# A graph layer on one core: the node features of every fifth group are loaded during the edge stage

## What is computed

```python
h = silu(edge_scalars @ Wfc1/4);  w = h @ Wfc2/8             # 192 weights per edge
e0, e1 = (x0 @ Wl1_0)[src], (x1 @ Wl1_1)[src]                # gathered source nodes
mid    = products of w, e0, e1 and the edge's 4 harmonics     # per edge
mean   = segment_sum(mid, dst) / max(count, 1)               # per node
conv   = mean @ Wl2_s, mean @ Wl2_v;  alpha = mean @ Wa
y      = x @ Wsc * node_vec1 + alpha * conv
out    = layernorm(x + y)                                    # 160 features per node
```

## Time and profile before

| | |
|---|---|
| median of 3 runs | 924.31 us (922.17 to 926.71) |
| the profiled execution's own time | 922.11 us |
| its span, first to last instruction | 920.4 us |
| busy: PE, DVE, ACT, POOL | 855.8, 808.2, 626.2, 714.1 us |
| data moved | 186.77 MB, mean 203 GB/s |
| edge stage, node stage | about 0 to 552 us, 552 to 920 us |

### The profile page before, as it was taken

One profiled execution on the slowest core, in us unless ns is written; L12 is line 12 of the kernel. 1 busy time (PEld: TensorE's weight loads), 2 busy tenths in 40 slices (PEclk: granted clock), 3 DMA queues, 4 the chain that ended last, 5 costly groups with the idle time before them and its releaser, 6 DMA issues.

```text
span 920.4 us, 32660 instructions
## 1 busy us (share of the span) xinstructions
PE 855.8 (93%) x10688; PEld 726.3 (79%) x10688; DVE 808.2 (88%) x2797; ACT 626.2 (68%) x1961; POOL 714.1 (78%) x804
## 2 busy tenths in 40 slices
PE   2999899999999999999999899989999999999994
PEld 1778778888877888888888778878888888888884
DVE  3788999999998999999999978888889898888897
ACT  1555555555555555555565546978988898888897
POOL 6777777777777776777777406989999998898995
PEclk9999999999999999999999999999999999999998
DMA  6465544544565555456544316999999999999994
GB/s 180 122 167 170 160 132 130 143 133 127 142 115 154 159 168 152 131 159 174 160 136 131 99 77 189 302 308 292 311 309 317 319 320 310 302 313 307 327 309 159
DMA packets 87539, 186.77 MB, mean 203 GB/s; under 512 B 17646, under 2 KB 48138, under 8 KB 87371
## 3 DMA queue, kind: packets, MB, share of 16 engines
q1 hardware_dynamic: 48411, 87.72, 29.4%
q10 hardware_dynamic: 20016, 61.15, 19.8%
q0 software_dynamic: 18944, 35.81, 17.7%
HBM read 119.66 MB, written 64.95 MB: 201 GB/s over the span
## 4 chain that ended last, share of the span: by engine, by line
PE 42%; DVE 14%; DMA 13%; issue 13%; SPq 9%; POOL 6%; ACT 1%; DVEq 0%; ACTq 0%; POOLq 0%
DMA win<-rows 10%; SPq L436 8%; PE ps L795 7%; PE ps L736 6%; POOL gat L587 6%; PE ps L715 5%; PE ps L733 4%; PE ps L696 4%; PE ps L702 4%; DVE mid L984 3%; DMA gat<-spread,srcs 3%; PE ps L678 3%; DVE z L1002 3%; PE ps L676 2%; PE ps L811 2%
## 5 line engine op out<-in xcount | busy, mean ns | idle before, releaser
L587 POOL DMA_INDIRECT gat<-turned,srcs x196 | 191.5, 977 | 67.0 <-issue 62.9
L587 POOL DMA_INDIRECT gat<-spread,srcs x196 | 188.2, 960 | 61.8 <-issue 59.1
L862 ACT ACTIVATE e_sb<-ps 128x512 f32<-128x512 f32 x196 | 106.4, 595 | 124.1 <-PE ps L702 124.1
L795 PE MATMUL ps<-win,hot 60*128 60x162 f32 x2352 | 189.1, 306 | 1.3 <-DVE hot L1325 1.1
L736 PE MATMUL ps<-wy,mid 128*128 128x161 f32 x784 | 182.3, 314 | 0.0
L795 PEld LDWEIGHTS ps<-win,hot 60*128 60x128 f32 x2352 | 165.0, 186 | 17.7 <-issue 12.1
L650 POOL TENSOR_TENSOR res<-agg,pre 128x640 f32<-128x640 f32 x98 | 151.8, 1549 | 30.7 <-ACT agg L907 30.4
L1008 DVE SCALAR_TENSOR_TENSOR msg<-ps,sha,z 128x161 f32<-128x161 f32 x392 | 151.0, 385 | 14.0
L907 ACT ACTIVATE agg<-ps,coef 128x160 f32<-128x160 f32 x392 | 124.7, 423 | 31.0 <-DVE coef L1365 30.3
L733 PE MATMUL ps<-wy,mid 128*128 128x97 f32 x784 | 141.4, 262 | 0.2 <-DVE mid L984 0.2
L984 DVE TENSOR_TENSOR mid<-ps,e_sb 128x512 f32<-128x512 f32 x196 | 133.1, 680 | 2.1 <-PE ps L715 2.1
(11 more groups left out here) (104 smaller groups left out, 1500.4 us busy)
## 6 DMA issues: line engine op xcount, KB each, us to landing
win<-rows SPq DMA_DIRECT2D x392, 114.6 KB, 4.1
rows<-msg SPq DMA_DIRECT2D x98, 326.0 KB
out<-fin ACTq DMA_DIRECT2D x47, 640.0 KB, 6.6
xin<-x_g ACTq DMA_DIRECT2D x92, 322.0 KB, 5.2
gat<-turned,srcs POOLq DMA_INDIRECT x196
gat<-spread,srcs POOLq DMA_INDIRECT x196
eas<-ea_t SPq DMA_DIRECT2D x7, 384.0 KB, 5.1
xin<-x_g SPq DMA_DIRECT2D x6, 322.0 KB, 4.1
```

The costliest lines, as they stand in the source:

```text
L587: pool.indirect_dma_start(out=gat[:, slot, first:first + of.shape[1]], out_offset=None, in_=of, in_offset=bass.IndirectOffsetOnAxis(ap=src ...
L795: last = nc.tensor.matmul(agg_ps[b1][:, 2 * h + k, 0:SW], hot[side(h), b1, k, c, :], win[side(h), (b - 1) % RING, k, c, 0:SW], start=c == ...
L862: nc.scalar.activation(e_sb[:, t, :], e_ps[:, t], ACT.Copy).then_inc(e_out[t], 1)
```

## The change

The x of every fifth group (g = 4, 9, ..., 94; 19 groups) gets a place of its own, `kept_x`, and is loaded by SP in the edge stage, one group at each i from 22 to 40, after the stores of that i. Other groups go on through the ring of six places of `xin`, counted by their rank among the groups that are not kept; ACT issues no x load in the step of a kept group. The space comes from laying node-stage tiles on edge-stage ones: `xa`, `hot`, `agg` and `xt` on `eas`, `res` and `pre` on `gat`, `fin` on the new tile `te`, which holds `t_sb` and `e_sb`. The edge-stage tables that lay in `res` and `fin` now lie in `kept_x`. No instruction of PE, DVE or POOL is added, removed or moved; POOL waits once for all kept loads (`kept_in`).

```diff
+KEEP = 5
...
+    KEPT = NG // KEEP
...
-        xa = sb("xa", [P, 2, GROUP + 1, P])
-        hot = sb("hot", [P, 2, 2, WC_ROWS, P])
-        agg = sb("agg", [P, 2, GROUP, D])
-        xt = sb("xt", [P, 2, GROUP + 1, P])
-        pre = sb("pre", [P, 2, GROUP, D])
-        res = sb("res", [P, RING, GROUP, D])
-        fin = sb("fin", [P, RING, GROUP, D])
+        kept_x = sb("kept_x", [P, KEPT, GROUP, XW])
...
+        def is_kept(g):
+            return g % KEEP == KEEP - 1
+
+        def rank(g):
+
+            return g - (g + 1) // KEEP
+
+        def of_rank(r):
+            return r + r // (KEEP - 1)
+
+        def x_tile(g):
+            return kept_x[:, g // KEEP] if is_kept(g) else xin[:, rank(g) % X_RING]
...
+            def keep_nodes(n):
+                sp.dma_start(kept_x[:, n].rearrange("p k w -> p (k w)"),
+                             block_rows(x_g, KEEP * n + KEEP - 1)).then_inc(kept_in, 16)
...
+                if 0 <= i - STARTS // 2 < KEPT:
+                    keep_nodes(i - STARTS // 2)
...
-                    n = (RING * i + b) % X_RING
-                    pool.wait_ge(x_in[n], 16 * ((RING * i + b) // X_RING + 1))
+                    g = RING * i + b
+                    x = x_tile(g)
+                    if is_kept(g):
+                        pool.wait_ge(kept_in, 16 * KEPT)
+                    else:
+                        pool.wait_ge(x_in[rank(g) % X_RING], 16 * (rank(g) // X_RING + 1))
...
-                if group_alive(i, b, 2) and group_alive(i, b, 2 - X_RING):
...
+                g = RING * i + b - 2
+                if group_alive(i, b, 2) and not is_kept(g) and of_rank(rank(g) + X_RING) < NG:
```

More of the change, by code:

```diff
@@ L109, in gnn_kernel @@
     CH = 4
-    assert NB - 1 >= WINDOWS + RING > EARLY + RING and WINDOWS > FLAG // 2 + 4 and NG // RING > 2 and NG % 2 == 0 and T <= 512 and NT < CH * P
+    KEPT = NG // KEEP
+    assert KEPT <= NB - 1 - STARTS // 2 and NB - 1 >= WINDOWS + RING > EARLY + RING and WINDOWS > FLAG // 2 + 4 and NG // RING > 2 and NG % 2 == 0 and T <= 512 and NT < CH * P
     inv8, inv32 = MUL0 ** -0.5, MUL1 ** -0.5
@@ L204, in gnn_kernel, with scratch @@
         shift = sb("shift", [P, RING, GROUP])
-        def scratch(tile, first, dims, dt=F32):
-            flat = tile[:].rearrange("p g k w -> p (g k w)")[:, first:first + dims[0] * dims[1]]
+        def scratch(first, dims, dt=F32):
+            flat = kept_x[:].rearrange("p g k w -> p (g k w)")[:, first:first + dims[0] * dims[1]]
             return flat.bitcast(dt).rearrange("p (a b) -> p a b", b=dims[1])
[L211 to L215, removed]
+        seq = scratch(0, (2, T), I32)
+        greater = scratch(2 * T, (1, T)).squeeze(1)
+        picked = scratch(3 * T, (CH, P), I32)
+        picked_below = scratch(3 * T + CH * P, (CH, P))
+        below = scratch(3 * T + 2 * CH * P, (CH, T))
+        t_sb = te[:, 0:12 * P].rearrange("p (b c k e) -> p b c k e", b=2, c=3, k=2)
+        e_sb = te[:, 12 * P:20 * P].rearrange("p (t e) -> p t e", t=2)
+        eas_flat = eas[:].rearrange("p b e -> p (b e)")
+        gat_flat = gat[:].rearrange("p n w -> p (n w)")
+        xa_at, hot_at = 0, 2 * (GROUP + 1) * P
+        agg_at = hot_at + 4 * WC_ROWS * P
+        xt_at = agg_at + 2 * GROUP * D
+        xa = eas_flat[:, xa_at:hot_at].rearrange("p (b k e) -> p b k e", b=2, k=GROUP + 1)
+        hot = eas_flat[:, hot_at:agg_at].rearrange("p (b k c e) -> p b k c e", b=2, k=2, c=WC_ROWS)
+        agg = eas_flat[:, agg_at:xt_at].rearrange("p (b k w) -> p b k w", b=2, k=GROUP)
+        xt = eas_flat[:, xt_at:xt_at + hot_at].rearrange("p (b k e) -> p b k e", b=2, k=GROUP + 1)
+        res = gat_flat[:, 0:RING * GROUP * D].rearrange("p (b k w) -> p b k w", b=RING, k=GROUP)
+        pre = gat_flat[:, RING * GROUP * D:(RING + 2) * GROUP * D].rearrange(
+            "p (b k w) -> p b k w", b=2, k=GROUP)
+        fin = te[:, 0:RING * GROUP * D].rearrange("p (b k w) -> p b k w", b=RING, k=GROUP)
         t_ps = ps[:, 0:2, 0:3 * P].rearrange("p k (c e) -> p k c e", e=P)
@@ L316, in gnn_kernel @@
         x_in = [sem(f"x_in{n}") for n in range(X_RING)]
+        kept_in = sem("kept_in")
         win_in = [sem(f"win_in{b}") for b in range(RING)]
@@ L418, in store_messages, with load_nodes @@
                     ).then_inc(messages_out[half], 16)
[L420 to L423, removed]
+            def load_nodes(r):
+                sp.dma_start(xin[:, r].rearrange("p k w -> p (k w)"), block_rows(x_g, of_rank(r))
+                             ).then_inc(x_in[r], 16)
+            def keep_nodes(n):
+                sp.dma_start(kept_x[:, n].rearrange("p k w -> p (k w)"),
+                             block_rows(x_g, KEEP * n + KEEP - 1)).then_inc(kept_in, 16)
             def load_windows(i, b):
@@ L1305, in step @@
                 scaling = group_alive(i, b, 5) and RING * i + b - 5 < NG - 3
-                nodes = (RING * i + b - 2) % X_RING
+                x = x_tile(RING * i + b - 2) if adding else None
                 g = groups(i, b, 2)
@@ L1352, in step @@
                         last = nc.vector.tensor_tensor(
-                            pre[:, b0, :, n:n + w], sc, xin[:, nodes, :, 1 + n:1 + n + w],
+                            pre[:, b0, :, n:n + w], sc, x[:, :, 1 + n:1 + n + w],
                             ALU.add)
```

18 lines of the change are left out of this document (8 added, 10 removed).

## The result

The changed kernel takes 917.49 us (median of 20 runs, 912.79 to 926.23), the kernel before 925.95 us (20 runs, 922.17 to 930.86). The ratio is 0.9925, with a 95% interval of 0.9902 to 0.9947. By it the changed kernel is 7 us faster (5 to 9); the two medians differ by 8.5 us. Forecast were 13.8 us (a ratio of 0.985).

What follows compares the result with a forecast made beforehand. The prediction took DMA bytes (3.52 us a group), just above PE's 3.45, to bound the node stage. A 14.3 us gain there less 0.5 us in the edge stage gave -13.8, from 924.3 to 910.5 us; range 906.0 (less 0.5) to 920.6.

Steps and rivals of the forecast that it cites:

- What remains of the stalls: Node stage: stalls left after the change, bounded by nothing and 6 us, taken as 4 us, for a gain of 14.3.
- DMA's is 3.52 us at best: Node stage: a group's 1127 kB at 320 GB/s need 3.52 us, against PE's own pace of 3.45 us.
- 13.8 us of ring against 4.1 us of landing: Node stage: a four-group window ring, 13.8 us at PE's pace, should carry 0.3 us, as windows land in 4.1 us (median).
- SP's short waits for PE: Node stage: SP waits for PE only 20.2 us in 322, so it issues windows soon after places come free.
- The first rival: Node stage: stalls are of latency, not bytes; only 3.7 us gained (920.6 us), or up to twice that; chance 0.20.
- The sentence at the end of the prediction: Node stage: prediction most wrong if engines fully busy at 320 GB/s merely had much queued, not because they could do no more.
- The edge stage: Edge stage: 19 added x loads cost nothing, or one wait of about 2.5 us at i = 22; 0.5 us taken.
- The lead of 8.7 us: Edge stage: a later gather ended 8.7 us before DVE took it, without a wait; most kept loads fall into that stretch.
- The tiles' new places: Node-stage tiles laid on edge-stage ones: no wait added, nothing counted, 1 us to either side for the turn between stages.
- ACT's 19 issues: Node stage: ACT issues 19 DMAs fewer, but at 3.26 of 3.45 us it does not end last; nothing counted.
- POOL as the next bound: Node stage, a rival: POOL's chain packs only into 3.53 us, losing 7.7 us, for 918 us; chance 0.06.
- The cap of 18.3 us: Node stage: the stalls are worth at most 18.3 us, as below that PE holds the pace at 3.45 us a group.

Runs made afterwards that it cites:

- e5: Changed kernel with no x loads in the node stage after groups 0 to 5; later groups all read group 4's x; ratio to the kernel before 0.9851.
- e11: Changed kernel storing only 32 of 1280 columns (16 KB, not 640 KB) for the first 94 groups; ratio to the kernel before 0.9808.
- e1: The changed kernel run once more, unedited, for a second trace; ratio to the kernel before 0.9931.
- e4: Changed kernel with one kept x load, at i = 30, in place of 19; all kept groups read it; ratio to the kernel before 0.9925.
- e13: Kernel before, nothing kept, with each group's output stored by itself and POOL waiting for the last label copy; ratio to the kernel before 0.9855.
- e3: Changed kernel making the 19 kept loads, but its node stage loads every group's x through the ring as before; ratio to the kernel before 1.0002.
- e14: Changed kernel with single stores, POOL waiting for the last label copy and kept loads at i = 24 to 42, second run; ratio to kernel before 0.9853.
- e9: Kernel before, nothing kept, with each group's output stored by itself (320 KB a step); ratio to the kernel before 0.9883.
- e2: Changed kernel with the kept loads issued two i later, at i = 24 to 42; ratio to the kernel before 0.9898.
- e7: Changed kernel with POOL making the first two groups' scaled x only after DVE's last edge-stage label copy; ratio to the kernel before 0.9889.

## Why the prediction was wrong

**The step that failed** is "What remains of the stalls": 4 us, between nothing and 6. Five traces show 12.7 us in the mean (7.3 to 18.8), so the node stage gained 5.5 us, not 14.3. The two bounds were both made of bytes over a rate, and the pace that they rest on, "DMA's is 3.52 us at best", was a reading of a busy share of 1.00 as a ceiling. In its place the runs show a path of 7.0 us, from PE's freeing of a place to DVE's copy, that SP's issuing and the landing share. The prediction had two things wrong in it. It set 13.8 us of ring against 4.1 us of landing, where 7.0 us were there and 2.7 of them went to SP. And it took SP's short waits for PE (20.2 us in 322) as a sign that SP issues in time; they go with an SP at work for 3.47 of 3.67 us a group.

The store of 640 KB every second group was in my text, as a reason to take 4 us and not 0. Split in two at the same bytes, it takes 12 us of stalls away (18.2 to 5.9 and 5.1; ratio 0.9883). But it is not the only cause: leaving out the x loads with the store as it was takes 13 away (e5), and leaving out most of the output takes them all (e11). Taking out one x load in five took 5.5 away, known to some 2 us from the scatter of its five traces.

**The first rival came closest**, with a time of 920.6 us, "or up to twice that" gain, 917 us; 917.5 us was measured. I gave it 0.20, since I let "the share is 1.00 at the highest rate" weigh against it. That row speaks for bursts just as well: the engines are busy while a burst drains. What it would show came only in part: window waits above 20 us in e1 and e4 (23.0 and 30.8), but 16.8 in the first trace, and shares of 0.93 to 0.95 where it wanted them visibly below 0.95. That it is the kept group's own step that is relieved was not tested. The sentence at the end of the prediction on what would make it wrong by most names this case.

The Trainium skill's figure of some 358 GB/s for a core ("DMA: Bandwidth & Descriptors", "Where 436 GB/s comes from") pointed the right way against my 320. My sentence that the trace does not reach it held only for the stretches in the earlier trace rows: the kernel before moves 345 GB/s over 10.5 us and 380 over 3.5 us, with loads and stores together, and there the measurement decides. The most over 581 to 884 us of a node stage is 326, in e13.

**The edge stage**: 0.5 us was taken for the loads; e3 gives 1.0002 +- 0.0027 (2.5 us), and e4, without 18 of them, has the same ratio as the changed kernel. Within that, it was right, by the reading of one load in the earlier trace rows. The lead of 8.7 us held too: no trace has a late gather after 294 us on account of a kept load. The prediction put a wait of up to 2.5 us at i = 22 down to the kept load. That wait is there without the load and scatters: 0.5 to 3.55 us near 280 us in 16 of the 17 traces, none over 0.4 us in e14. Just before it, from 270 to 275 us, the DMA engines are full at 54 GB/s while the table of starts is written; that this is what holds the gathers up was not tested. What the prediction missed is that a stall can cost TensorE's clock on top.

**The tiles' new places** at nothing: right, by e3, within 2.5 us. **ACT's 19 issues** at nothing: no run has them alone. **POOL as the next bound**: not so at 3.45 us; in e11 all groups but one follow each other at that pace with POOL in the loop. **The cap of 18.3 us**: right; e11 reaches it.

What stays open: by what a store issued by ACT lengthens SP's issues one to three microseconds later (the records show that it does), and why the same traffic stalls for 7.3 us in one trace and 18.8 in another. Of the last 5 us with single stores it is known that the windows land late where DVE waits for them (5.7 us on average in e9, 5.6 in e13), but not why.

## What to carry to other kernels

In this kernel a busy share of 1.00 over the DMA engines said that transfers were queued, not that the bytes were too many: it stood at 54 and at 345 GB/s alike. So before bytes are moved away, split the largest burst and see what the same bytes cost. Price a wait by its whole path, from the place that comes free to the first use, and count the issuing engine's own time in it: short waits of that engine can mean that it is full. Look for stalls at a DMA share below 1, too. One trace of a stall can be far from the next: the same traffic gave 7 and 19 us here, so take a second before a term is fitted to it.

## What the runs showed of the hardware that I had not expected

- A stall of PE of 1.72 (e11) to 3.47 us (e2) was followed in some executions by half the clock for 3.4 or 6.8 us, and in others, of 1.98 and 2.20 us (before) and 2.83 us (e1), by none. In e4 it made one group's matmuls 3.14 us, not 1.93.
- A DVE copy between SBUF tiles of 128x4 elements took 2.57 us while POOL ran two tensor_tensor pairs, and 0.16 us when POOL waited (e7).
- SP's issue of one window DMA takes 0.33 us or, most often behind a store, up to 2.42 us (before, 581 to 884 us). Bytes moved per busy time rise a little when the stores are single: 323 GB/s at a share of 0.99 and 326 at 1.00 (e9, e13), against 311 to 312 at 0.98 in two traces of the kernel before.
- SP's register load of four window starts takes 0.58 us at the median and up to 1.74 us in the kernel before, at most 0.80 us in e11.
